# A vision tower's first scan stage: the image quarters' tokens normalised apart, and the stage prepared by chunks between patch matmuls

## The reference

```python
h = tokens(x, W)                        # patches (T x 768) @ W.T -> T x 192
x = layernorm(h)
for way in ("fwd", "bwd"):              # Mamba, both ways over the 49 tokens of an image
    xc, z = split(x @ W_in.T)           # 384 channels each
    u = silu(conv_b + conv4(xc))
    dtr, B, C = split(u @ W_x.T)        # 12, 16 and 16 columns
    dt = softplus(dtr @ W_dt.T + b_dt)
    s = exp(dt * A) * s + dt * u * B    # 16 states for each channel, token after token
    y = (sum_n s * C + u * D) * silu(z)
    out += y @ W_out.T
h = h + layernorm(out + x) * g + b
```

## Time and profile before

| | |
|---|---|
| time, median of 3 runs (least to most) | 1539.99 us (1538.18 to 1540.39) |
| time of the profiled execution | 1541.07 us |
| its span, first to last instruction | 1539.1 us |
| granted TensorE clock, mean | 0.944 of 2.4 GHz |
| PE busy | 1345.3 us (87%) |
| DVE busy | 903.4 us (59%) |
| ACT busy | 668.8 us (43%) |
| POOL busy | 558.7 us (36%) |
| DMA | 151.95 MB, mean 99 GB/s |

### The profile page before, as it was taken

One profiled execution on the slowest core, in us unless ns is written; L12 is line 12 of the kernel. 1 busy time (PEld: TensorE's weight loads), 2 busy tenths in 40 slices (PEclk: granted clock), 3 DMA queues, 4 the chain that ended last, 5 costly groups with the idle time before them and its releaser, 6 DMA issues.

```text
span 1539.1 us, 18449 instructions
## 1 busy us (share of the span) xinstructions
PE 1345.3 (87%) x6708; PEld 773.4 (50%) x6708; DVE 903.4 (59%) x1488; ACT 668.8 (43%) x1193; POOL 558.7 (36%) x400
## 2 busy tenths in 40 slices
PE   6889898988989878649988859989999999999998
PEld 6544454544545434326443345547856658344444
DVE  2249999999999999983100038865446625121122
ACT  2478677776767664232110016641542251213311
POOL 0248988889898987500000020012034302000000
PEclk9879999999999999958998979999999999899999
DMA  6041422405041331072999950000010001021101
GB/s 200 11 159 33 138 76 93 136 33 168 12 159 53 117 106 62 8 300 79 399 396 398 396 148 1 1 1 0 1 37 1 2 1 37 1 86 35 36 0 32
DMA packets 41332, 151.95 MB, mean 99 GB/s; under 512 B 10364, under 2 KB 17659, under 8 KB 37020
## 3 DMA queue, kind: packets, MB, share of 16 engines
q1 hardware_dynamic: 37148, 149.21, 27.3%
q10 hardware_dynamic: 4096, 1.58, 0.4%
HBM read 147.56 MB, written 1.63 MB: 97 GB/s over the span
## 4 chain that ended last, share of the span: by engine, by line
PE 54%; DVE 20%; issue 11%; DMA 5%; ACT 5%; POOL 4%; SPq 0%; ACTq 0%; DVEq 0%; POOLq 0%
PE ps L1720 52%; DVE arena L1325 7%; DVE arena L1314 5%; DMA arena<-in_e_b 5%; POOL arena L785 3%; ACT arena L878 2%; ACT ps L925 1%; DVE stats L1263 1%; PE ps L1729 1%; DVE arena L1603 1%; POOL arena L790 1%; DVE arena L1362 1%; DMA arena<-in_patches 1%; DVE arena L1358 1%; DVE arena L1334 1%
## 5 line engine op out<-in xcount | busy, mean ns | idle before, releaser
L1720 PE MATMUL ps<-arena 128*98 128x192 f32 (+14 forms) x5260 | 963.2, 417 | 106.0 <-DVE arena L1368 20.0
L1720 PEld LDWEIGHTS ps<-arena 128*98 128x98 f32 (+12 forms) x5260 | 544.6, 154 | 498.6 <-issue 297.9
L785 POOL TENSOR_TENSOR arena<-arena 128x784 f32<-128x784 f32 x192 | 367.9, 1930 | 81.9 <-DVE arena L1325 81.3
L1720 PE MATMUL ps<-arena,ident 128*128 128x392 f32 x900 | 351.9, 521 | 51.2 <-POOL arena L785 42.9
L1325 DVE TENSOR_TENSOR_SCAN arena<-ps,arena 128x784 f32<-128x784 f32 x192 | 341.0, 1776 | 0.4 <-ACT ps L925 0.4
L1720 PEld LDWEIGHTS ps<-arena,ident 128*128 128x128 f32 x900 | 170.4, 197 | 201.0 <-POOL arena L785 73.2
L925 ACT ACTIVATE ps<-arena 128x384 f32<-128x384 f32 x384 | 207.8, 574 | 118.4 <-DVE arena L1325 117.7
L878 ACT ACTIVATE arena<-ps 128x392 f32<-128x392 f32 (+9 forms) x265 | 124.2, 487 | 290.2 <-PE ps L1720 224.3
L878 ACT ACTIVATE arena<-ps,arena 128x392 f32<-128x392 f32 (+2 forms) x194 | 105.2, 602 | 235.8 <-PE ps L1720 149.6
L1314 DVE TENSOR_TENSOR arena<-ps,arena 128x784 f32<-128x784 f32 x192 | 182.8, 952 | 10.1 <-ACT ps L940 9.9
L1466 DVE COPY arena<-ps 128x384 f32<-128x384 f32 x32 | 16.3, 552 | 151.1 <-PE ps L1937 151.1
(11 more groups left out here) (178 smaller groups left out, 848.4 us busy)
## 6 DMA issues: line engine op xcount, KB each, us to landing
arena<-in_e_w SPq DMA_DIRECT2D x32, 2304.0 KB
arena<-bc_rows SPq DMA_DIRECT2D x128, 392.0 KB, 4.7
arena<-in_patches SPq DMA_DIRECT2D x4, 1176.0 KB, 12.4
arena<-comb_rows SPq DMA_DIRECT2D x1, 3136.0 KB, 10.7
arena<-in_mlp_w SPq DMA_DIRECT2D x5, 576.0 KB, 4.3
arena<-arena ACTq DMA_DIRECT2D x128, 12.0 KB, 8.2
arena<-in_mlp_w SPq DMA_DIRECT2D x5, 384.0 KB, 3.6
arena<-in_mlp_w SPq DMA_DIRECT2D x10, 192.0 KB, 4.0
```

Of the source, the lines that this page charges most:

```text
L785: pool.tensor_tensor(pair(hbuf[:, at % SLOTS, :]), pair(hbuf[:, at % SLOTS, :]), c_all[:, n:n + 2, :], ALU.mult).then_inc(times_c, 1)
L1720: return pe.matmul(dst, lhsT, rhs, start=first, stop=last)
```

## The change

It does the following.

- The patches are laid out by quarter in DRAM, so that a quarter is one run of 9408 bytes in each partition. Loads are in a new order: patch weights, quarter 0, the ten small loads, quarter 1, forward weights, quarters 2 and 3, the rest. The quarters lie in other places: 0 and 1 under `b_all` and the first part of `c_all`, 3 under its last part, 2 under `hbuf`. The row loads begin after tile 7; the load of C rows for pair 5 of stage 0 waits for the last tile, and DVE waits for tile 11 before it writes `hbuf`.
- ACT makes all 30 diagonals before it copies tile 0.
- DVE normalises tiles 0 to 3 and 4 to 7 ahead of the loop. The statistics of tiles 8 to 15 are made by DVE at unit 8, and ACT normalises them at unit 10 (`NORM_DVE`, `NORM_ACT`). POOL adds their bias row after the loop.
- Stage 0 has a program of its own. PE: tiles 0 to 6, the transposes of quarter 0, tile 7, the three `xc`, the three convolutions, tile 8, `proj`, three `step`, tiles 9 to 15. ACT and DVE do tanh and product by chunks; only chunk 0 goes all the way to du before unit 0. The rest of chunks 1 and 2 is done at units 2 (squares, ACT) and 3 (series on DVE, dt and du on POOL). Tiles 12 to 15 are copied out by ACT at units 0 and 1, and PE's tile 14 needs the bank of tile 12.
- What stood ahead of unit 0 for later work moves into the 24 units of stage 0 (`EARLY`): z of stage 0 at units 1 to 7, and the whole of stage 1, whose du is made at unit 22 and copied at unit 23. The transposes of quarters 1, 2 and 3 stand at units 5, 25 and 48.

```diff
+EARLY = {
+    0: {"z_pe": (25, 26, 27), "z_act": (27, 28, 29), "tanh_z_act": (30, 31), "silu_z_pool": (31, )},
+    1: {"xc_pe": (0, 1, 2), "xc_act": (2, 3, 4), "conv_pe": (4, 6, 8), "conv_act": (6, 8, 9), "tanh_act": (9, 10),
+        "silu_pool": (10, ), "proj_pe": (11, ), "proj_act": (12, ), "step_pe": (12, 12, 13), "step_act": (13, 13, 14),
+        "exp_act": (15, ), "ln_act": (16, ), "inverse_act": (17, ), "s_pool": (17, ), "square_act": (19, 20, 21),
+        "series_dve": (20, 21), "dt_pool": (21, ), "du_pool": (22, ), "z_pe": (13, 17, 22), "z_act": (15, 19, 25)},
+    2: {"xc_pe": (-10, -9, -8), "xc_act": (-7, -6, -5), "conv_pe": (-6, -4, -2), "conv_act": (-4, -2, 0)}}
+TOK_ACT = {0: (12, 13), 1: (14, 15)}
+REST_SQUARE, REST_SERIES, REST_POOL = 2, 3, 3
+NORM_DVE, NORM_ACT = 8, 10
-LATE_TURN_PE, LATE_TURN_ACT = (1, 4), (4, 7)
-DIAG_ACT = (-28, -21)
-SCHEDULE = range(-UNITS - 12, LOOPED + 14)
+LATE_TURN_PE, LATE_TURN_ACT = (5, 25, 48), (7, 28, 50)
+SCHEDULE = range(-1, LOOPED + 14)
...
+            load("tok_w", w_tok, a["tok_w"])
+            patch_load(0)
             for r, p in enumerate(("fwd", "bwd")):
                 load("small", taps[r], a[f"{p}_conv_w"])
...
+            patch_load(1)
+            mamba_load(0)
+            patch_load(2)
+            patch_load(3)
...
-            diagonals(tap_diag, 0, tap_of(0), 3 * TAPS)
-            for i in range(NT):
+            for r in range(2):
+                diagonals(tap_diag, r, tap_of(r), 3 * TAPS)
+                diagonals(skip_diag, r, skip_of(r), 3)
...
+            s_st.wait_taken(act, 2)
+            own.then(act.activation(e_t, e_t, ACT.Exp, scale=-1.0))
+            act.wait_ge(first_products, 3)
+            own.then(act.activation(g_t, e_t, ACT.Ln, bias=act_c[:, 0:1]))
+            act.activation(g_t[:, 0:1], g_t[:, 0:1], ACT.Exp, scale=-1.0).then_inc(r_ready, 1)
+            act.activation(g_t[:, 1:3], g_t[:, 1:3], ACT.Exp, scale=-1.0).then_inc(r_ready, 1)
+            act.wait_ge(first_products, 4)
+            series_squares(slice(0, 1), 0)
+            for i in range(9, TOK_LATE):
+                token_out(i)
...
+            dve.wait_ge(r_ready, 1)
+            TT(e_t[:, 0], e_t[:, 0], g_t[:, 0], ALU.mult).then_inc(first_products, 1)
+            own.then(first_series(slice(0, 1), 0))
+            TT(dt[:, 0, 0], dt[:, 0, 0], relu_t[:, 0], ALU.add).then_inc(first_products, 1)
+            dve.wait_ge(first_products, 5)
+            TT(du[:, 0, 0], dt[:, 0, 0], xconv[:, 0, 0], ALU.mult).then_inc(first_products, 1)
+            s_xhT.wait_taken(dve, 1)
+            s_tok.wait_filled(dve, TOK_LATE - 1)
...
+                if at == REST_SERIES:
+                    first_series(slice(1, 3), 2).then_inc(l_ready, 1)
+                if at == NORM_DVE:
+                    late = slice(2 * TQ, NT)
+                    norm_stats(h, range(2 * TQ, NT), lambda i: s_tok.wait_taken(dve, i))
...
+            for i in range(2 * TQ - 1):
+                token(i)
+            pe.wait_ge(const_ready, 1)
+            turned_xh(range(2))
+            token(2 * TQ - 1)
+            for c in range(3):
+                inner(s_xc, c, 128 * c, 0)
             pe.wait_ge(xc_edges, 1)
+            for c in range(3):
+                convolved(0, c)
+            token(8)
+            projected(0, lambda c: pe.wait_ge(first_products, c + 1))
+            for c in range(3):
+                stepped(0, c)
+            for i in range(9, NT):
+                token(i)
```

More of the change, by code:

```diff
@@ L79, with due @@
 GAPPED = QI * (TOKENS + 1)
-LATE_TURN_PE, LATE_TURN_ACT = (1, 4), (4, 7)
-DIAG_ACT = (-28, -21)
-SCHEDULE = range(-UNITS - 12, LOOPED + 14)
-def due(at, slot):
-    ahead, off = divmod(at - slot, UNITS)
-    return ahead + 1 if off == 0 and 0 <= ahead + 1 < STAGES else None
+LATE_TURN_PE, LATE_TURN_ACT = (5, 25, 48), (7, 28, 50)
+SCHEDULE = range(-1, LOOPED + 14)
+TIMES = {}
+for _s in range(STAGES):
+    for _name, _slots in SLOT.items():
+        if _s > 0 or _name not in HEAD:
+            for _k, _slot in enumerate(EARLY.get(_s, {}).get(_name, _slots)):
+                assert (_name, _k, UNITS * (_s - 1) + _slot) not in TIMES
+                TIMES[_name, _k, UNITS * (_s - 1) + _slot] = _s
+def due(at, name, k=0):
+    return TIMES.get((name, k, at))
 class Stage:
@@ L212, in build_tower @@
         K = Region(46674)
+        w_tok = K.take(128, [PATCH_CHUNKS, D])
         b_row = K.take(TILE, [D])
@@ L905, in turned_xh, with xc_out, conv_out @@
                 copy_out(s_xhT, i, xhT[:, c, quarter(q)], bank(s_xhT.banks[i][0], CH, 0, QT))
-            for i in range(4):
-                turned_xh(i)
+            def xc_out(s, c):
+                i = 3 * s + c
+                copy_out(s_xc, i, xc[:, c, :, TAPS - 1:TAPS - 1 + TOKENS],
+                         steps_of(bank(s_xc.banks[i][0], 128, 0, QT)))
+            def conv_out(s, c):
+                i = 3 * s + c
+                copy_out(s_cv, i, xconv[:, s % 2, c, :], bank(s_cv.banks[i][0], 128, 0, QT),
+                         ACT.Identity, bias=conv_b[s % 2][:, c:c + 1])
@@ new lines, in proj_out, with step_out, series_squares @@
+            def proj_out(s):
+                copy_out(s_xp, s, proj, bank(s_xp.banks[s][0], 64, 0, QT))
+            def step_out(s, c):
+                i, b_c = 3 * s + c, dt_b[s % 2][:, c:c + 1]
+                s_st.wait_filled(act, i)
+                src = bank(s_st.banks[i][0], 128, 0, QT)
+                act.activation(relu_t[:, c, :], src, ACT.Relu, bias=b_c)
+                act.activation(e_t[:, c, :], src, ACT.Abs, bias=b_c).then_inc(s_st.taken["act"], 1)
+            def series_squares(some, n):
+                own.then(act.activation(g_t[:, some], e_t[:, some], ACT.Square))
+                act.activation(dt[:, 0, some], g_t[:, some], ACT.Square, scale=ATANH_Z, bias=act_c[:, 1:2])\
+                    .then_inc(q_ready, 1)
+                act.wait_ge(q_ready, n + 1)
+                act.activation(g_t[:, some], g_t[:, some], ACT.Square, scale=ATANH_Z, bias=act_c[:, 2:3])\
+                    .then_inc(q_ready, 1)
@@ new lines, in _ @@
+            for i in range(2 * TQ - 1):
+                token_out(i)
+            for i in range(2):
+                turned_xh(i)
+            token_out(2 * TQ - 1)
+            for c in range(3):
+                xc_out(0, c)
+            for c in range(3):
+                conv_out(0, c)
+                s_cv.wait_taken(act, c)
+                own.then(act.activation(g_t[:, c], xconv[:, 0, c], ACT.Tanh, scale=0.5))
+                act.activation(g_t[:, c], g_t[:, c], ACT.Identity, scale=0.5, bias=act_c[:, 3:4])\
+                    .then_inc(tanh_ready, 1)
```

335 lines of the change are left out of this document (192 added, 143 removed).

## The result

The changed kernel takes 1531.59 us (1524.11 to 1533.44, 13 runs) beside 1538.7 us (13 runs) of the kernel before: ratio 0.9948, 95% interval 0.9931 to 0.9965, 8.0 us less (5.4 to 10.6). It is faster, as forecast, but by 8 us and not 20, and lies above the 1513 to 1527 of the forecast's own case, inside the range but near its upper end.

The account below looks back on a forecast made before the run. A serial chain of waits was taken to bound the kernel up to the first scan, DVE from there. 42.1 us gained at the start less 21.8 in stage 0 gave 20.3 us less, so 1520 us, range 1507 to 1533.

Parts of the forecast that it names:

- the forecast's own case: Whole kernel: a time of 1513 to 1527 us, given a chance of 0.50.
- First matmul: Start of the kernel: PE's first matmul at 8.3 us, 6.4 us sooner, with 7.3 and 10.0 kept in the range.
- pieces of the start: Up to the first scan: four stretches shortened, so the scan starts at 60.1 us, 42.1 us sooner.
- Stage 0: First stage of the scan: 88.2 us against 66.4, plus 21.8, from DVE's work, du and waits.
- DVE's own work: Stage 0: 65.3 us busy plus 1.95 for series and 5.6 for late statistics, 72.9 us.
- The du wait: Units 22 and 23: POOL's du of stage 1 and ACT's copy delay scan 23, plus 5.3 us, uncovered.
- The waits: Stage 0: DVE waiting behind late ACT and PE; 12.3 us walked, 10.0 taken, 0 to 20 in the range.
- Covered: Work said to cost nothing: POOL's late bias adds behind the loop (4 us if uncovered), transposes' copies, C rows of pair 5.
- B: Rival: start gains 38 us, stage 0 takes 97 to 100; 1532 to 1535 us; chance 0.20 for 1527 to 1537.
- A: Rival: ACT stays ahead, stage 0 costs only DVE's work and the wait for du, 78.2 us; 1510 us; chance 0.22.
- C: Rival: PE cools down in stage 0, which takes 122 us at a share of 0.7; 1554 us; chance 0.05.
- The sum: Whole kernel: 42.1 us gained at the start less 21.8 lost in stage 0, 20.3 us less.

Follow-up runs that it names:

- e5: Changed kernel with the two series steps of chunks 1 and 2 at units 3 and 4, POOL's dt and du at unit 4; stage 0 96.23 us.
- e2: Changed kernel with stage 1's du of chunk 0 made by DVE after scan 22, POOL making only chunks 1 and 2; stage 0 92.75 us.
- e1: Changed kernel with POOL's eight late bias adds at units 28 to 35, not behind the loop; 1528.54 us, ratio 0.9925 to the kernel before.
- e6: Changed kernel with statistics of tiles 8 to 15 at unit 22, normalising at 25, quarter 2's transposes at 29; stage 0 93.66 us, stage 1 70.28.
- e7: Changed kernel with statistics of tiles 8 to 15 left out, their factors taken from tiles 0 to 7; stage 0 92.78 us.

## Why the prediction was wrong

**First matmul, pieces of the start: right.** Each piece of the sum came within 1.3 us, the whole within 0.9: 41.2 us for 42.1. The diagonals did set the pace, as the step had it. The measured time lies in the range; its low end should by its own sum (1540 less 31.3) have been 1509 and not 1507.

**Stage 0: the sum that failed, by 8.0 us in four terms.** It came out at 96.2 and not 88.2 us. By the scans' starts DVE loses 34.8 us over 24 units of 2.56, where the forecast's terms leave 26.7:

| term | foretold | measured |
|---|---|---|
| series of chunks 1 and 2, statistics (units 3 and 8) | 7.55 | 3.44 + 6.34 = 9.8 |
| du (unit 22) | 5.3 | 7.0 |
| waits behind ACT and PE (units 1, 2, 6, 12 to 14, 16, 19) | 10.0 | 11.9, of them 1.7 at unit 1 |
| DVE's other work in the loop | 65.3 - 61.4 = 3.9 | 4.6 (series of stage 1) + 1.5 (units 9, 10, 17) = 6.1 |

*DVE's own work.* The series and the statistics are there, but 2.5 us of port lock lie in them (1.5 at unit 3, 1.0 at unit 8). I had put these into the range only. Unit 8's part rested on POOL being nearly idle there, and it was not: it ended a product at 95.4. e5 shows that unit 3's part hides in the wait between scans 6 and 7, as the step said, so taking it away alone does not shorten the stage.

*The du wait: mis-sized.* POOL was a whole product behind: its product of unit 21 took 2.90 us, held up by DVE's series step, and dt came behind it. The step counted POOL from scan 22 as if it were free. e2 took 2.3 us of the wait away.

*The waits: right in kind.* I walked 12.3 us and took 10.0. Measured are 1.7 + 1.5 + 1.5 + 4.4 + 1.65 + 1.0 = 11.9 us. This looks as if the walk held and the deduction did not, but the 1.7 us at unit 1 are there only when PE's clock falls at 60 us; without them it is 10.1. Single entries were off by up to 1.3 us (2.8 foretold at unit 6, 1.54 measured), so the agreement of either sum is in part luck.

*The base: a term put at nothing without a reason.* I started from DVE's busy time of 65.3 us and not from the stage's 66.4, so the 1.1 us that DVE already waited there were dropped, and the new small waits with them. Here the loss over the sum is 2.3 us.

**"Covered": the step whose mechanism was wrong.** I wrote that POOL's eight late bias adds "begin behind its last product at 643.3 us and end at about 647.4" and are needed at 653.78. They ended in time (635.2, and the steps that need them come behind 645), and they still cost 3.5 us (e1): not by being late, but by what they do to DVE while they run (2.4 us) and, behind it, to PE's clock (1.1). The earlier trace rows already had it: the step of 0.95 us at 642.41, beside POOL's last product. The text used that row for units 3 and 8 and not for the one place where new POOL work was put beside a run of such steps. The Trainium skill's rule on a DVE instruction with two SBUF inputs beside a GpSimd instruction that reads SBUF (SBUF — State Buffer, "Who interferes with whom") was cited for units 3 and 8 alone. The trace agrees with it here too, at 0.15 us without POOL and 0.45 beside it.

**Rivals.** B (1532 to 1535; 0.20 with what lies between it and the forecast) came nearest, by its second half: stage 0 at 96 us, but with the start intact. A was wrong: ACT did not stay ahead. C did not decide: PE's clock in stage 0 is 0.93, with falls to 0.72 at 60 to 64 us and 0.50 at 100 to 104. The first costs 1.7 us at unit 1, and by execution it comes or stays away. The second is absent in e6 and e7, where other things differ too, so its price isn't shown.

**The sum.** 42.1 - 21.8 = 20.3 was foretold; 41.2 - 29.8 + 0.6 - 3.5 = 8.5 came. Of the 11.8 us between, 8.0 are stage 0, 3.5 the loop's end, 0.9 the start, less 0.6 in the stages between.

What stays open: how the waits for ACT, 10.1 us without unit 1, would fall if stage 1's steps stood in other units (e7 shows that of 4.2 us taken from DVE at unit 8 only 1.8 are gained), and what part of them behind unit 1 is PE's clock. No run changed these slots alone. The terms from e2, e5, e6 and e7 rest on one execution each.

## What to carry to other kernels

Work moved out of a serial start into a loop is paid there at the price of the busiest engine's order, not of its free time: here 33 us of earlier start bought 0.2 us, and the loads' new layout and order alone bought 8.3. When an instruction of POOL is moved to a place where it is "hidden", look at what DVE does in that place: here a chain of eight small two-operand steps was slowed threefold by the adds beside it. Start a sum from the stage's length and not from the busy time of its bound. And before a gain of 2 us is put down to an edit, compare the units ahead of the edit, where the code is the same: here they differed by 1.7 us with PE's clock.

## What the runs showed of the hardware

A POOL add of 98x192 elements (0.49 us) holds up a DVE step on 64x1 elements by 0.30 us, eight times in a row. PE then stood for 3.7 us and not 1.4, its mean clock over the stretch was 0.79 and not 1.00, and its 38 matmuls took 11.1 us and not 8.7. After one and the same idle of 3.79 us PE's clock fell in one execution (0.72 from 60 to 64 us) and stayed at 1.00 in another (e2). The lock goes both ways (POOL's product of 143.13 took 2.90 us beside DVE's series step, for 1.85), and it takes single-input steps too where they have several elements: the `tensor_scalar` on 98x8 took 1.12 us at 94.31 and its like 2.61 us in e6, for 0.17; on 64x1 elements `tensor_scalar` (L1357, 0.15 us at 630.08) ran undisturbed beside the POOL product that ended at 631.4, and the two-input step behind it waited for that product's end (0.94 us at 630.44). The Trainium skill's section names both kinds: two SBUF inputs, and copies or `tensor_scalar` in a two-port mode; the trace is in line with that, and my prediction used only the first. The four patch loads with one piece of 9408 bytes a partition are issued in 0.43 us each, or a little less, where the four of before, with six pieces each, took 7.25 us together; what stood in the queue ahead of them differed too.
